# A state-space layer with new slot tables for each engine, and norm, delta copy and last bias on ScalarE

## What is computed

```python
h = layernorm(x) * (1 + ca) + sa
x_and_res = h @ in_proj_w                 # 128 -> 2 * 256
xp, res = x_and_res[..., :256], x_and_res[..., 256:]
h = silu(causal_conv(xp, 4 taps) + conv_b)
dlt, Bm, Cm = split(h @ x_proj_w, (64, 16, 16))
delta = softplus(dlt @ dt_proj_w + dt_proj_b)
deltaA = exp(delta[..., None] * A)        # 256 channels x 16 states
deltaB_u = (delta * h)[..., None] * Bm[:, :, None, :]
state_t = deltaA_t * state_{t-1} + deltaB_u_t
y_t = sum over the 16 states of state_t * Cm_t, plus h * D
x = x + ga * ((y * silu(res)) @ out_proj_w)
h = layernorm(x) * (1 + cb) + sb
x = x + gb * (h @ (W + lora).T + b)
```

## Time and profile before

| what | us |
|---|---|
| median of 3 runs (lowest, highest) | 5793.53 (5793.14, 5795.39) |
| the profiled execution's own time | 5792.16 |
| its span, first to last instruction | 5790.3 |
| busy: PE, DVE, ACT, POOL | 5207.9, 4944.2, 4116.4, 3339.1 |
| mean granted TensorE clock | 0.962 of full speed |

### The profile page before, as it was taken

One profiled execution on the slowest core, in us unless ns is written; L12 is line 12 of the kernel. 1 busy time (PEld: TensorE's weight loads), 2 busy tenths in 40 slices (PEclk: granted clock), 3 DMA queues, 4 the chain that ended last, 5 costly groups with the idle time before them and its releaser, 6 DMA issues. The chain is left out here.

```text
span 5790.3 us, 112187 instructions
## 1 busy us (share of the span) xinstructions
PE 5207.9 (90%) x34984; PEld 3808.2 (66%) x34984; DVE 4944.2 (85%) x8818; ACT 4116.4 (71%) x12293; POOL 3339.1 (58%) x2277
## 2 busy tenths in 40 slices
PE   7999899999999999999999999999999996667666
PEld 6999766776676766767767666677676774333333
DVE  4666689999999999999999999999999994787877
ACT  3555478888788788788888887878878785544543
POOL 1222266666666666676666766766667662443444
PEclk9999899999999999999999999999999997788887
DMA  1000000000000000000000000000000000000000
GB/s 21 4 4 3 24 1 1 0 0 10 11 0 0 0 13 8 0 0 6 14 1 0 0 6 15 0 0 0 10 5 0 0 0 5 1 3 3 2 3 4
DMA packets 35422, 25.54 MB, mean 4 GB/s; under 512 B 11315, under 2 KB 29302, under 8 KB 35190
## 3 DMA queue, kind: packets, MB, share of 16 engines
q1 hardware_dynamic: 26302, 22.22, 1.3%
q10 hardware_dynamic: 8888, 0.45, 0.1%
HBM read 20.57 MB, written 2.10 MB: 4 GB/s over the span
## 5 line engine op out<-in xcount | busy, mean ns | idle before, releaser
L1145 POOL TENSOR_TENSOR b_w<-b_w,b_vt 128x512 f32<-128x512 f32 x768 | 980.0, 1276 | 1276.8 <-DVE b_vt L1054 646.6
L1149 POOL TENSOR_TENSOR b_rn<-b_ssm,all_neg_half 128x16 f32<-128x16 f32 x384 | 1126.9, 2935 | 32.0
L971 ACT ACTIVATE b_PT<-ps 128x512 f32<-128x512 f32 x768 | 461.0, 600 | 434.4 <-PE ps L826 433.7
L1080 DVE TENSOR_REDUCE b_nm<-ps 128x4 f32<-128x640 f32 x768 | 631.0, 822 | 95.1 <-PE ps L806 85.2
L953 ACT ACTIVATE b_Pr<-ps,b_nm 128x128 f32<-128x128 f32 x1536 | 564.0, 367 | 179.0 <-DVE b_nm L1080 176.6
L874 PE MATMUL ps<-b_Whi,b_xlo 128*128 128x512 f32 x1152 | 584.7, 508 | 40.9 <-DVE b_vt L1054 27.9
L955 ACT ACTIVATE b_Pr<-ps,b_nm 128x160 f32<-128x160 f32 x1536 | 610.0, 397 | 0.0
L1052 DVE TENSOR_TENSOR b_w<-ps,until_b_rotab 128x512 f32<-128x512 f32 x768 | 529.4, 689 | 25.0 <-ACT b_sq L986 7.5
L986 ACT ACTIVATE b_sq<-ps 128x512 f32<-128x512 f32 x768 | 467.1, 608 | 82.3 <-PE ps L876 81.9
L1054 DVE TENSOR_TENSOR b_vt<-ps,until_b_rotab 128x512 f32<-128x512 f32 x768 | 523.2, 681 | 0.0
L1056 DVE TENSOR_REDUCE b_ss<-b_sq 128x8 f32<-128x512 f32 x768 | 519.7, 677 | 0.0
(11 more groups left out here) (256 smaller groups left out, 13996.5 us busy)
## 6 DMA issues: line engine op xcount, KB each, us to landing
b_Wraw<-in_L_ffn_Wqkv SPq DMA_DIRECT2D x36, 256.0 KB, 2.8
b_Wo<-in_L_ffn_Wo SPq DMA_DIRECT2D x6, 512.0 KB, 4.0
a_xtok<-in_L_attn_hidden_states SPq DMA_DIRECT2D x16, 128.0 KB, 2.1
out<-c_xout SPq DMA_DIRECT2D x16, 128.0 KB, 1.8
b_W<-in_L_ffn_W SPq DMA_DIRECT2D x6, 341.0 KB, 2.9
setup_wmod<-in_L_wmod SPq DMA_DIRECT2D x2, 384.0 KB
b_W<-in_L_ffn_W SPq DMA_DIRECT2D x6, 128.0 KB
setup_rot<-in_rot SPq DMA_DIRECT2D x1, 256.0 KB
```

The costliest lines, as they stand in the source:

```text
L1080: nc.vector.tensor_reduce(s.nm[:, 2 * p:2 * p + 2], ps[:, S_BANK[0]:S_BANK[1] + 1, 0:TT * KEYS].rearrange("p j (t k) -> p j t k", t=TT), A ...
L1145: nc.gpsimd.tensor_tensor(rows, rows, s.vt[:, i % 4], ALU.add).then_inc(s.pool_add, 1)
L1149: nc.gpsimd.tensor_tensor(s.rn[:, j], s.ssm[:, j], g.neg_half[:, 0:HB], ALU.pow).then_inc(s.pool_r, 1)
```

## The change

The shared slot table goes. Each engine gets tables of its own, for each piece and each pair, and the order of the pieces inside a slot is another one on each engine. The pairs of GpSimd change from B 3, 4, 6 and C 1, 3, 5 to B 0, 3, 4 and C 1, 3, 4. Its powers and products have slots of their own (`POOL_AT`, `POOL_STATS1`, `POOL_STATS2`): products B0 and B3, then the first norm's power; B4; C1; copy of x3 and the second norm's power; C3; C4.

```diff
-B_SLOT = {i: i for i in range(PAIRS)}
-SCAN_SLOT = {5: 0, 9: 1}
-C_SLOT = {8 + i: i for i in range(PAIRS)}
-SUM_LAG = 10
-
-X3_SLOT, X3_TR_SLOT, X3_TOK_SLOT, STATS1_SLOT, NORMED1_SLOT, H_TR_SLOT, HT_SLOT, IN_SLOT, XP_SLOT, CONV_SLOT, SILU_SLOT = 0, 2, 3, 4, 6, 9, 9, 9, 12, 14, 14
-XD_SLOT, SPLIT_XD_SLOT, DL_SLOT, Z_SLOT, SOFTPLUS_SLOT, DELTA_SLOT = 0, 1, 3, 3, 5, 8
-Y_SLOT, OP_SLOT, X4_SLOT, X4_TR_SLOT, X4_TOK_SLOT, STATS2_SLOT, NORMED2_SLOT, H2_TR_SLOT, HT2_SLOT, LIN_SLOT, X5_SLOT = 1, 5, 5, 6, 9, 9, 10, 12, 14, 15, 15
-OUT_SLOT_C, XOUT_SLOT = 2, 2
-POOL_B, POOL_C = (3, 4, 6), (1, 3, 5)
+POOL_B, POOL_C = (0, 3, 4), (1, 3, 4)
 N_POOL = len(POOL_B) + len(POOL_C)
 DVE_B = [i for i in range(PAIRS) if i not in POOL_B]
 DVE_C = [i for i in range(PAIRS) if i not in POOL_C]
-FACTOR_SLOT = {9: (0, 7), 10: (7, 14), 11: (14, 20), 12: (20, 26), 13: (26, 32)}
+PRODUCTS = [(False, i) for i in POOL_B] + [(True, i) for i in POOL_C]
+PE_B = {0: (0, 1), 1: (2, 3), 3: (4,), 8: (5,), 9: (6,), 10: (7,)}
+PE_C = {6: (0,), 9: (1, 2), 11: (3,), 12: (4, 5), 13: (6, 7)}
+PE_SUM = {10: (0,), 11: (1,), 13: (2,), 14: (3,), 17: (4, 5), 18: (6,), 24: (7,)}
+PE_OUT, PE_XD, PE_X3, PE_DL, PE_OP, PE_X4, PE_H, PE_IN, PE_H2, PE_CONV, PE_LIN = 7, 0, 7, 3, 9, 9, 10, 11, 11, 12, 12
+DVE_B_AT = {0: (1,), 3: (2,), 7: (5,), 8: (6, 7)}
+DVE_C_AT = {6: (0,), 11: (2,), 13: (5, 6), 15: (7,)}
+DVE_SCAN = {4: 0, 12: 1}
+DVE_X3, DVE_XD, DVE_Y, DVE_STATS1, DVE_X4, DVE_DELTA, DVE_STATS2, DVE_X5 = 3, 3, 5, 6, 7, 5, 8, 13
+ACT_ROWS = {0: (0,), 1: (1,), 3: (2,), 9: (3,), 12: (4,), 15: (5,)}
+ACT_OUT, ACT_X3, ACT_Z, ACT_SOFTPLUS, ACT_X4, ACT_APPLY1, ACT_HT, ACT_XP, ACT_APPLY2, ACT_HT2, ACT_SILU, ACT_DLT, ACT_LIN = 2, 2, 1, 2, 10, 6, 11, 11, 11, 11, 15, 0, 15
+FACTOR_SLOT = {4: (0, 2), 10: (2, 8), 11: (8, 20), 12: (20, 27), 15: (27, 32)}
+POOL_AT = {1: (0, 1), 5: (2,), 9: (3,), 13: (4,), 14: (5,)}
+POOL_X3, POOL_STATS1, POOL_STATS2 = 12, 1, 12
```

Three pieces go from VectorE to ScalarE. The norm is computed as `rstd * x + shift` with `shift = -mean * rstd`; the negation is new on VectorE, the product for the shift new on GpSimd:

```diff
+    nc.vector.tensor_scalar_mul(ln.negm[:], ln.mv[:, :, 0], -1.0).then_inc(ln.var_ready, 1)
...
+def layernorm_pool_c(nc, pool, ln, g, n):
+    pool.wait_ge(ln.var_ready, n + 1)
+    nc.gpsimd.tensor_tensor(ln.rstd[:], ln.var[:], g.neg_half[:, 0:TT], ALU.pow).then_inc(ln.rstd_ready, 1)
+    pool.wait_ge(ln.rstd_ready, 2 * n + 1)
+    nc.gpsimd.tensor_tensor(ln.shift[:], ln.negm[:], ln.rstd[:], ALU.mult).then_inc(ln.rstd_ready, 1)
...
+def layernorm_apply_c(nc, act, ln, src, n):
...
+    act.wait_ge(ln.rstd_ready, 2 * n + 2)
+    for tt in range(TT):
+        last = nc.scalar.activation(ln.xn[:, tt], src[:, tt], ACT.Identity, bias=ln.shift[:, tt:tt + 1], scale=ln.rstd[:, tt:tt + 1])
```

The delta copy and the last bias:

```diff
-                        nc.vector.tensor_copy(s.dlt[RANK_ROWS], ps[RANK_ROWS, G_BANK, 0:NT]).then_inc(s.xd_ready, 1)
...
-                        nc.vector.tensor_scalar(s.tmp[:], ps[:, TAIL_BANK, 0:NT], g.blin[:], s.md_tail[:, 3:4], ALU.add, ALU.mult).then_inc(s.tmp_ready, 1)
-                        dve.wait_ge(s.tmp_ready, t + 1)
-                        nc.vector.tensor_tensor(s.x5T[:], s.tmp[:], s.x4T[:], ALU.add).then_inc(s.x5_ready, 1)
...
+                        dve.wait_ge(s.tmp_ready, t + 1)
+                        nc.vector.scalar_tensor_tensor(out=s.x5T[:], in0=s.tmp[:], scalar=s.md_tail[:, 3:4], in1=s.x4T[:], op0=ALU.mult, op1=ALU.add).then_inc(s.x5_ready, 1)
...
+                    if step.tail and slot == ACT_LIN:
+                        act.wait_ge(s.lin_full, t + 1)
+                        nc.scalar.activation(s.tmp[:], ps[:, TAIL_BANK, 0:NT], ACT.Identity, bias=g.blin[:]).then_inc(s.tmp_ready, 1)
...
+                    if step.delta and slot == ACT_DLT:
+                        act.wait_ge(s.xd_full, f + 1)
+                        nc.scalar.activation(s.dlt[RANK_ROWS], ps[RANK_ROWS, G_BANK, 0:NT], ACT.Copy).then_inc(s.xd_ready, 1)
```

More of the change, by code:

```diff
@@ L1506, in body @@
+                    if step.store and slot == PE_OUT:
                         pe.wait_ge(s.x5_ready, u + 1)
                         transpose_tokens(TAIL_BANK, by_tile(s.x5T)).then_inc(s.out_full, 1)
-                    if step.delta and slot == XD_SLOT:
-                        pe.wait_ge(s.h_ready, f + 1)
-                        for c in range(CC):
-                            last = nc.tensor.matmul(ps[:, G_BANK, 0:NT], s.Wx[:, c], s.h[:, other, c], start=c == 0, stop=c == CC - 1)
-                        last.then_inc(s.xd_full, 1)
@@ L1513, in body @@
-                    if step.inner and slot == X3_TR_SLOT:
-                        pe.wait_ge(s.x3_ready, m + 1)
-                        wait(pe, s.gate_ready, m)
-                        transpose_tokens(F_BANK, by_tile(s.x3T)).then_inc(s.x3_full, 1)
-                    if step.delta and slot == DL_SLOT:
-                        pe.wait_ge(s.xd_ready, f + 1)
-                        for c in range(CC):
-                            last = nc.tensor.matmul(ps[:, G_BANK, c * NT:(c + 1) * NT], s.Wdt[RANK_ROWS, c * P:(c + 1) * P], s.dlt[RANK_ROWS], start=True, stop=True)
-                        last.then_inc(s.dl_full, 1)
@@ L1523, in body @@
+                    if step.tail and slot == PE_OP:
                         wait(pe, s.xout_ready, t)
@@ L1543, in body @@
-                    if step.inner and slot == H_TR_SLOT:
-                        pe.wait_ge(s.l1.normed, m + 1)
-                        transpose_tokens(F_BANK, s.l1.xn, NT).then_inc(s.h_full, 1)
-                    if step.inner and slot == IN_SLOT:
+                    for at, item, there in ((slot, n, step.states), (slot + SLOTS, t, step.tail)):
+                        for i in PE_SUM.get(at, ()) if there else ():
+                            if i == 0:
+                                wait(pe, s.y_ready, item)
+                            wait_yc(pe, item, i)
+                            for k in (2 * i, 2 * i + 1):
+                                last = nc.tensor.matmul(ps[:, Y_BANK], g.ident[:], s.bu[:, :, k], start=k == 0, stop=k == NS - 1, skip_group_check=True)
+                            if i == 0:
+                                for c in range(CC):
+                                    nc.tensor.matmul(ps[:, Y_BANK, c * NT:(c + 1) * NT], s.D_diag[:, c], s.h[:, own if at < SLOTS else other, c], start=False, stop=False, skip_group_check=True)
+                            if i == PAIRS - 1:
+                                last.then_inc(s.y_full, 1)
@@ L1547, in body @@
+                    if step.inner and slot == PE_IN:
                         if step.delta:
@@ L1562, in body @@
                         last.then_inc(s.conv_full, 1)
[L1563 to L1565 removed]
+                    if step.tail and slot == PE_X4:
+                        pe.wait_ge(s.x4_ready, t + 1)
+                        transpose_tokens(TAIL_BANK, by_tile(s.x4T)).then_inc(s.x4_full, 1)
             phase_c_steps(pe, body)
```

296 lines of the change are left out of this document (154 added, 142 removed).

## The result

The changed kernel takes 5603.0 us in the median of four runs (5599.0 to 5603.8), against 5794.1 (5793.1 to 5795.4) for the kernel before in four runs: 191 us less, ratio 0.9658 with a 95% interval of 0.9624 to 0.9693. 5608 had been predicted. The profiled execution took 5603.8 us with a span of 5602.0, so the spans differ by 188.3 us. Where they went is read in three cuts: up to the first scan, from there to the last second scan, and the end.

What follows compares the result with a forecast made beforehand. Waits between engines, none full, were taken to bound the state-space layer. Thirteen intervals of 12.4 us (161), the last two 10 and 6, the end 7 and first steps 1 gave 185 us: 5608 us forecast, range 5570 to 5700.

Steps and rivals of the forecast that it cites:

- What bounds the kernel: State-space layer: no engine full, VectorE 80% busy; a chain of waits crossing engines fills 55.4 us per step.
- Step of 43.0 us: One full step, first scan to next: 43.0 us including 0.8 for issue gaps, 12.4 less than before.
- the walk: One full step traced through all engines' new queue orders with trace durations; next first scan at 42.2 us before gaps.
- The last wait: Ahead of the next first scan: held by GpSimd's product B3, which ends at 42.2 us.
- The sum: Whole kernel: savings over intervals, last steps, end and first steps, 185 us in all.
- The thirteen intervals: Intervals between steps in the state-space layer: 12.4 us saved in each, 161 us together.
- The last two: Last two intervals, with no new input and less for TensorE and ScalarE: gains of about 10 and 6 us.
- a gain of 1: First steps: ScalarE's extra order costs about 1 us, the first scan without a product beside it gains 2.
- the end: Behind the last scan: y's wait of 18 us falls to 10.5, less 0.5 for the shift, a gain of 7.
- Moved work: Norms, delta copy and last bias leave VectorE, 4.7 and 0.9 us a step; VectorE falls from 44 to 36 us.
- The caught power: Rival, 20%: GpSimd's second power waits behind the second scan; 6.1 us per step, 49 in place of 43, 5692 us.
- TensorE's low clock: Rival, 3%: TensorE at 1.2 GHz after gaps becomes the bound; step 66 us at clock 0.5, about 5940 us.

Runs made afterwards that it cites:

- tables_only: The changed kernel with its slot tables and queue orders, but norms, delta copy and last bias back on VectorE: 5637.5 us, ratio 0.9727.
- c_first: The changed kernel with TensorE's sum of pair 2 moved behind the spreads of C6 and C7: 5603.1 us, ratio 0.9669.
- b01: The changed kernel with GpSimd making B0 and B1 instead of B0 and B3, and VectorE taking pair 3: 5592.6 us, ratio 0.9653.
- moves_only: The kernel before with its old tables and pair sets, but norms, delta copy and last bias moved to ScalarE: 5819.4 us, ratio 1.0043.
- scan1_shared: The changed kernel with two spare GpSimd products of 128x512 behind B3, to fall beside the first scan: 5615.7 us, ratio 0.9695.
- power2_later: The changed kernel with two spare GpSimd products, 128x1024 and 128x768, ahead of the second norm's power: 5716.8 us, ratio 0.9863.
- power2_late: The changed kernel with one spare GpSimd product of 128x1024 ahead of the second norm's power: 5614.7 us, ratio 0.9697.

## Why the prediction came out right

- **What bounds the kernel.** It held that no engine is full and that waits between engines make the step. Tables alone, with not one instruction fewer on VectorE, gave 157 us (tables_only), and 97 of the 101 us of VectorE's idle time that went are one wait for TensorE.
- **Step of 43.0 us.** 41.9 measured over twelve full intervals. In a step of 43.0 the walk's eight times come 0.6 to 1.4 us later than it said, which is about the 0.8 us that it added at the end for gaps. In the other nine the output projection, the shift, the factors, the second norm and the convolution end 0.3 to 1.1 us ahead of the walk, and the next scan starts at 41.0 to 42.2, where the walk without its 0.8 had 42.2. The last wait is the one that it named, B3 on GpSimd (c_first, b01), by 0.3 to 0.9 us over VectorE's own work. The delta wait of 1.58 us, for which the walk had 0.3, is in three steps only.
- **The sum.** 188.3 us against 185, and its terms erred against each other, so that the total is nearer than its parts: that is luck. The thirteen intervals gained 176 us, not 161: the first 14.7 (53.2 to 38.5), twelve full ones 13.4 each (55.3 less 41.9) instead of 12.4. The last two gained 13.1 and 1.1 (55.56 to 42.44, 45.7 to 44.6) instead of 10 and 6. One loss was not in the sum at all: in the last step the second scan stands 20.2 us behind the first instead of 13.2, 7 us lost, as in the new order three of VectorE's B pairs (before: one), the gate product, x4 and the second norm's statistics are between them there too. The first scan starts 1.0 later instead of a gain of 1, and the end gained 5.8 instead of 7. 176 + 14.2 - 7.0 - 1.0 + 5.8 = 188. The range's lower end doesn't follow from the step that it names: 40.5 us a step give 5608 - 13 x 2.5 = 5575, not 5570.
- **Moved work.** A norm costs ScalarE 0.48 busy and 0.44 net (0.87 for two) instead of 0.38; the negation 0.41 in the mean instead of 0.1, from 0.16 alone, and the 1.31 us that it takes in six of the twelve full steps put the second scan 1.15 us later, which the walk didn't have; the shift 0.20 instead of 0.25. VectorE is busy 37.1 us in the step instead of 36: the walk let no VectorE instruction meet GpSimd's B0 and B3, and x3 (1.07 instead of 0.48) and small ones do. C3 was held as forecast: the four products of C3 and C4 take 7.21, which leaves 4.7 for C3.
- **The split of the gain.** The walk couldn't give it. Of its 8 us a step taken from VectorE, those of the moves do not pay by themselves (moves_only +25 us, with the norm placed well -7), and pay fully only with the tables (34.0 us off VectorE, 37.9 off the stretch).
- **Rivals.** The caught power is real, was farther away than the rival had it (the power starts 2.06 us ahead of the scan; the 0.7 is what the walk had left behind the shift's end, and measured 1.1), and was underpriced: 9.2 us per step, not 6.1, mostly as the low clock that follows the gap was left out. TensorE's low clock decided nothing: the clock rose to 0.85, with the output projection (2.05 us for four matmuls, 1.13 before) still at the low level behind 3.6 us of idle, as forecast (granted 0.50 from 5219 to 5225). How much of the tables' 157 us is collisions and how much is the order of the queues was not separated by a run: VectorE's stretched instructions are 48 us of tables_only's shorter stretch, but what they and GpSimd's caught ones cost through the waits is not known. Scan1_shared puts the price of two products beside the first scan at 0.8 us a step, and 8 of TensorE's 12.1 us a step of waiting for the norm were its place in the queue.

## What to carry to other kernels

Walk one full step of the pipeline through all queues with the durations of the trace before moving anything: it came within 3% of the step's length, and named the wait that ends last. Work taken off the busiest engine turns into time only if that engine's waits are short; a move that puts a waiting instruction in front of other work on the receiving engine can lose more than it frees. Keep short GpSimd instructions on a chain out of the reach of long VectorE ones, and know the margin in microseconds, counted to their start.

## What the runs showed of the hardware that was not expected

- A two-column instruction is not a cheap one. The 128x2 negation on VectorE took 0.16 us in 25 of 32 cases and 1.31 in seven, where it met the border of two GpSimd products; the 128x2 shift on GpSimd took 0.20 alone and 3.73 or 4.18 when a half scan ran.
- The spare GpSimd products took 1.04 us for 128x512 (scan1_shared, the one that starts ahead of the scan), 1.46 for 128x768 (power2_later) and 1.89 for 128x1024 (power2_late): 0.85 us per 512 columns and 0.19 on top, an estimate from these three. The kernel's own products of 128x512 take 1.25. So power2_late's delay was 0.6 us short of the 2.5 expected mainly because a spare product is shorter than a product of the kernel (0.2 us per 512 columns); why it is, no run shows.
- Two GpSimd products beside the scan pair lengthen it by 1.6 us, but take 6.15 themselves instead of 2.1 (1.04 and 5.16, the second held until the first half scan had ended): at this border GpSimd loses more than VectorE.
